# One transformer layer with a routed feed-forward part: another staging of routing, experts and last phase, with GpSimd issuing the experts' row transfers

## The reference

```
h = layernorm(x) * (1 + ca) + sa
x = x + ga * attention(h)                      # one head of 128, softmax over 2048 keys
h = layernorm(x) * (1 + cb) + sb
shared   = (silu(h @ Wg.T) * (h @ Wu.T)) @ Wd.T          # inner width 512
probs    = sigmoid(h @ R.T + bias)             # 8 experts, the two best, scores normed to 1
combined = sum over the two of score_e * expert_e(h)     # each expert like shared, own weights
out = x + gb * (shared + combined)
```

## Time and profile before

| | before |
|---|---|
| median of 3 runs | 1787.32 us |
| profiled execution | 1788.52 us |
| its span, first to last instruction | 1786.8 us |
| TensorE busy | 1645.2 us, 92% |
| VectorE busy | 1046.3 us, 59% |
| ScalarE busy | 826.2 us, 46% |
| GpSimd busy | 497.9 us, 28% |
| granted TensorE clock, mean | 0.965 of full |
| DMA | 134.34 MB, 75 GB/s |

### The profile page before, as it was taken

How to read it: one execution, slowest core, us unless ns; L and a number is a source line. 1 busy time by engine, 2 the same in 40 slices (tenths; PEclk the granted TensorE clock), 3 DMA queues, 4 the chain that set the end, 5 groups by cost and what they waited for, 6 DMA issues and landing times. The chain is left out here.

```text
span 1786.8 us, 34539 instructions
## 1 busy us (share of the span) xinstructions
PE 1645.2 (92%) x10888; PEld 1492.6 (84%) x10889; DVE 1046.3 (59%) x2242; ACT 826.2 (46%) x1628; POOL 497.9 (28%) x504
## 2 busy tenths in 40 slices
PE   8899999999999959897609999999999999988997
PEld 7899999999999848797508888888888888877886
DVE  6777777777778757576533333333333333338987
ACT  5566666565655545455203333333333333335553
POOL 4423223222000030654751020111022400007775
PEclk9999999999999969999859999999999999999999
DMA  3211111111011060211252121122122111114544
GB/s 113 95 43 42 42 42 45 40 47 37 25 37 36 25 230 7 89 73 60 104 192 99 53 88 56 53 91 88 54 90 90 53 53 56 53 43 122 159 144 139
DMA packets 102463, 134.34 MB, mean 75 GB/s; under 512 B 11620, under 2 KB 89572, under 8 KB 102252
## 3 DMA queue, kind: packets, MB, share of 16 engines
q1 hardware_dynamic: 85948, 86.56, 14.8%
q0 software_dynamic: 15312, 44.58, 7.5%
q10 hardware_dynamic: 1120, 2.10, 0.3%
HBM read 79.71 MB, written 53.49 MB: 75 GB/s over the span
## 5 line engine op out<-in xcount | busy, mean ns | idle before, releaser
L794 DVE TENSOR_TENSOR e_aT_lo<-e_bank,e_aT_hi 128x512 fp32r<-128x512 f32 x136 | 94.1, 692 | 239.2 <-ACT e_aT_hi L781 239.2
L757 PE MATMUL e_bank<-e_w_hi,e_xT_hi 128*128 x544 | 225.9, 415 | 0.0
L757 PE MATMUL e_bank<-e_w_hi,e_xT_lo 128*128 x544 | 214.0, 393 | 0.0
L757 PE MATMUL e_bank<-e_w_lo,e_xT_hi 128*128 x544 | 213.3, 392 | 0.0
L800 DVE TENSOR_TENSOR e_prod<-e_silu_g,e_bank 128x512 f32<-128x512 f32 x136 | 93.6, 688 | 189.9 <-PE e_bank L757 189.9
L1394 ACT ACTIVATE e_y<-e_bank 128x256 f32<-128x256 f32 x136 | 52.2, 384 | 320.8 <-PE e_bank L33 320.8
L1565 POOL DMA_INDIRECT y<-y_rows,place_i x128 | 131.7, 1029 | 218.1 <-POOLq L1253 179.4
L608 DVE TENSOR_REDUCE bmax<-s_pair 128x1 f32<-128x512 f32 (+1 forms) x192 | 166.1, 866 | 12.1 <-PE s_pair L33 9.1
L346 ACT ACTIVATE pT_hi<-t_pair 128x512 fp32r<-128x512 f32 (+1 forms) x192 | 136.0, 749 | 78.6 <-PE t_pair L470 76.8
L627 DVE TENSOR_TENSOR pT_lo<-t_pair,pT_hi 128x512 fp32r<-128x512 f32 (+1 forms) x192 | 160.1, 862 | 17.5 <-ACT pT_hi L346 15.5
L339 ACT ACTIVATE prob<-s_pair,negmax 128x1024 f32<-128x1024 f32 x128 | 141.7, 1116 | 57.1 <-DVE negmax L620 51.2
(11 more groups left out here) (294 smaller groups left out, 4562.9 us busy)
## 6 DMA issues: line engine op xcount, KB each, us to landing
e_h<-x_rows SPq DMA_DIRECT2D x136, 128.0 KB, 2.0
y_rows<-e_y SPq DMA_DIRECT2D x136, 128.0 KB, 1.7
XS<-in_x SPq DMA_DIRECT2D x32, 256.0 KB, 2.7
XR<-in_x SPq DMA_DIRECT2D x32, 256.0 KB, 2.6
x<-XR SPq DMA_DIRECT2D x32, 256.0 KB, 2.1
out<-Z SPq DMA_DIRECT2D x16, 512.0 KB
Z<-x SPq DMA_DIRECT2D x2, 2048.0 KB, 15.6
e_w_raw<-in_gate_w POOLq DMA_DIRECT2D x7, 512.0 KB, 4.2
```

The costliest lines, as they stand in the source:

```text
L757: mm = pe.matmul(out[:, 0:I], l, w, start=(c == 0 and k == 0), stop=(c == HC - 1 and k == 2))
L794: dve.tensor_tensor(flat(aT_lo, par), a_bank[:, 0:I], flat(aT_hi, par).bitcast(F32), ALU.subtract).then_inc(f.aT_lo_done, 1)
```

## The change

Attention gets side work. All 27 weight matrices of the feed-forward parts (3 shared, 24 of experts, `piece` = 1024 columns each) are loaded by SP, split by GpSimd and stored, high and low, to HBM (`w_parts`). Statistics are joined on VectorE and made into reciprocal deviations on GpSimd, batch by batch (three of four within attention).

The shared phase loads its split weights. `h` is written by VectorE straight into one of four slots of rows, each row now 260 long: 256 features, the token's number, the place of its first choice, and two numbers for its score. There are eight groups of four steps. Eight further steps with one tile each do the shared part of tiles 32 to 39; within them VectorE makes the plan and SP writes the pad rows and loads the first expert's weights.

In the experts phase SP loads weights already split. GpSimd starts the load of each block's rows and scatters each block's result, in one order. VectorE copies the four extra columns (`rides`) and works out where each result goes and its score (`tell`); ScalarE multiplies by the score as it evicts. Results go to `y_rows` by token, so the last phase reads them with plain DMAs. There, GpSimd adds the two and gates, four tiles at a time, and VectorE adds to the residual; 24 steps remain.

```diff
@@ attention_phase, SP
+            def load_piece(i):
+                if i:
+                    sp.wait_ge(piece_out, 32 * i)
+                sp.dma_start(piece_raw[:], d.matrices[i]).then_inc(piece_in, 16)
+
+            def store_piece(i):
+                sp.wait_ge(piece_split, 2 * i + 2)
+                o = W * (i % 3)
+                for part, src in enumerate((piece_hi[:].bitcast(F32), piece_raw[:])):
+                    sp.dma_start(d.w_parts[i // 3, :, part, o:o + W], src).then_inc(piece_out, 16)
...
             for G in range(ALL):
                 if has_m(G + NG + 3):
                     chunk(G + NG + 3)
+                if 0 <= G - 2 < PIECES:
+                    store_piece(G - 2)
+                if 0 <= G - 1 < PIECES:
+                    load_piece(G - 1)
                 if G >= 2:
                     store(sp, G - 2)
@@ attention_phase, GpSimd
+            def split_piece(i):
+                pool.wait_ge(piece_in, 16 * i + 16)
+                pool.tensor_copy(piece_hi[:], piece_raw[:]).then_inc(piece_split, 1)
+                pool.wait_ge(piece_split, 2 * i + 1)
+                pool.tensor_tensor(piece_raw[:].bitcast(F32R), piece_raw[:], piece_hi[:].bitcast(F32),
+                                   ALU.subtract).then_inc(piece_split, 1)
@@ shared_phase, SP: weights
+            for k in range(3):
...
+                for part in range(2):
+                    o = 3 * W * part + W * k
+                    sp.dma_start(d.w_shared[:, o:o + W].bitcast(F32), d.w_parts[0, :, part, W * k:W * k + W]
+                                 ).then_inc(w_loaded[2 + k], 16)
@@ shared_phase, VectorE
+            def shift(m):
                 dve.wait_ge(scaled_done, m + 1)
...
+                g = m // GS
+                if m < STEPS and m % GS == 0 and g >= RING:
+                    dve.wait_ge(sent[g % RING], ONCE * (g // RING))
+                dve.tensor_tensor(rows_at(m), scaled[:, m % 2, 0:streams(m), :], both_halves(m, H),
                                   ALU.add).then_inc(f.rows_ready, 1)
...
+                if n % GS == 0 and 0 < n <= STEPS:
+                    place(n // GS - 1)
+                if n % GS == GS - 1 and n < STEPS:
+                    choose(n // GS)
+                if n == STEPS:
+                    dve.tensor_copy(free_i[:], base[0:1, GROUPS, :]).then_inc(free_known, 1)
+                if n == STEPS + 2:
+                    plan_ends()
+                if n == STEPS + 3:
+                    plan_experts()
+                if n == STEPS + 4:
+                    plan_rows()
@@ experts_phase, SP
+            for e in range(1, E):
+                if e >= 2:
+
+                    end = sp.value_load(d.ends_i[0:1, e - 2:e - 1], min_val=1, max_val=NBLK)
+                    hold(sp, d, f.y_mm, end)
+                    sp.wait_ge(d.w_ready, 16 * e)
+                sp.dma_start(d.w_all[:, e % 2, :].bitcast(F32), d.w_parts[e + 1].rearrange("p a n -> p (a n)")
+                             ).then_inc(d.w_ready, 16)
@@ experts_phase, GpSimd
+            def scatter(m, par):
+                if inside(m - 1, NBLK):
+                    hold(pool, d, y_sent[1 - par], 16 * half(m - 1, 1 - par) + 16)
+                hold(pool, d, f.y_out, m + 1)
+                pool.indirect_dma_start(d.y_rows, bass.IndirectOffsetOnAxis(ap=goes_to[:, par, :], axis=0),
+                                        y[:, par, :], None).then_inc(y_sent[par], 16)
 
             def load(m, par):
+                row = pool.value_load(d.table[0:1, 0, at(m)], min_val=0, max_val=d.all_rows - P)
+                pool.dma_start(h[:, par, :], d.x_rows[ds(row, P), :]).then_inc(h_in[par], 16)
 
             def step(n, par):
                 if inside(n + 2, NBLK):
+                    pool.wait_ge(ride_done, n + 1)
+                    hold(pool, d, f.xT_mm, n + 1)
                     load(n + 2, par)
                 if inside(n - 2, NBLK):
+                    scatter(n - 2, par)
@@ experts_phase, VectorE, after the products of step n: tell(n - 1), rides(n + 1)
+            def rides(m, par):
...
+                dve.wait_ge(h_in[par], 16 * half(m, par) + 16)
+                dve.tensor_copy(ride[:, par, :], h[:, par, H:H + 4]).then_inc(ride_done, 1)
@@ last_phase, GpSimd
+            for k, q in enumerate(order):
+                y1, y2 = y[:, k % RING, 0, :], y[:, k % RING, 1, :]
+                pool.wait_ge(y_in[k % RING], 32 * (k // RING + 1))
+                pool.tensor_tensor(y1, y1, y2, ALU.add).then_inc(summed, 1)
+                pool.wait_ge(summed, k + 1)
+                pool.tensor_tensor(tiles(y1), tiles(y1), gate_row(C * q).unsqueeze(1).to_broadcast([P, C, H]),
+                                   ALU.mult).then_inc(gated_done, 1)
@@ last_phase, VectorE
+            def output(k):
+
+                q = order[k]
+                dve.wait_ge(gated_done, k + 1)
+                if C * q >= EARLY:
+                    dve.wait_ge(shared_done, C * q - EARLY + C)
+                own = d.Z[:, C * q:C * q + C, :]
+                dve.tensor_tensor(own, own, tiles(y[:, k % RING, 0, :]), ALU.add).then_inc(out_done, 1)
```

More of the change, by code:

```diff
@@ L832, in shared_phase @@
     STEPS = d.steps
-    CHUNK = TB // 2
+    ALL = STEPS + d.extra
+    GROUPS = len(d.groups)
+    GS = STEPS // GROUPS
+    RING = d.ring
+    NBLK = d.blocks
+    W = d.piece
+    ROW = d.row
     Z, rows = d.Z, d.mod_rows
@@ L1174, in choose @@
                 op(dve.reciprocal(two_d(total), two_d(total)))
-                for k, best in enumerate((best1, best2)):
-                    op(dve.tensor_tensor(halves(d.score[:, k, :], first, size), best[:, own], total[:, own], ALU.mult))
+                op(dve.tensor_tensor(two_d(gap), two_d(best1), two_d(best2), ALU.subtract))
+                op(dve.tensor_copy(ride(g, 0), in_group(d.tokens[:], first, size)))
+                op(dve.tensor_tensor(ride(g, 2), best2[:], total[:], ALU.mult))
+                op(dve.tensor_tensor(ride(g, 3), gap[:], total[:], ALU.mult))
                 assert r[0] == ROUTE * g + SCORED
@@ L1226, in _ @@
-            scale(1, 1, 0)
-            shift(1, 1, 0)
-            f.dve_rows_low(dve, 0, 0)
-            for n in range(2, NB):
-                offsets(n, ORDER[n])
-            for g, (first, size) in enumerate(d.groups):
-                now[0] = first // CHUNK
-                pairs(dve, g, step, place)
-                choose(g)
-            place(len(d.groups) - 1)
-            f.dve_products_low(dve, STEPS - 1, 1)
-            for n in (STEPS - 2, STEPS - 1):
-                gated(n, n % 2, n // TB)
-                shared_out(n, n % 2)
@@ L1250, in experts_phase @@
+            f.dve_products_low(dve, ALL - 1, 1)
+            for n in (ALL - 2, ALL - 1):
+                gated(n)
+                shared_out(n)
+def experts_phase(nc, d):
+    E, I, W = d.E, d.I, d.piece
+    H = d.row - 4
+    HC, IC = H // P, I // P
     NBLK = d.blocks
-    W = HC * I
+    T = P * d.NT
     with ExitStack() as ctx:
@@ L1388, in _ @@
+            steps(pool, step)
+            scatter(NBLK - 2, 0)
+            scatter(NBLK - 1, 1)
+            for s in y_sent:
+                pool.wait_ge(s, 16 * (NBLK // 2))
         @block.scalar
@@ L1466, in _ @@
-            op(dve.tensor_reduce(nblocks[:], over[:], AX_X, ALU.add))
-            op(dve.tensor_copy(ends[:], nblocks[:]))
-            for e in range(1, E):
-                op(dve.tensor_tensor(ends[:, e:e + 1], ends[:, e - 1:e], nblocks[:, e:e + 1], ALU.add))
-            op(dve.memset(starts[:, 0:1], 0.0))
-            op(dve.tensor_copy(starts[:, 1:E + 1], ends[:]))
-            op(dve.scalar_tensor_tensor(out=shift[:], in0=starts[:], scalar=-float(P), in1=d.first_row[:, 0:E + 1],
-                                        op0=ALU.mult, op1=ALU.add))
@@ L1509, in _ @@
             f.dve_products_low(dve, NBLK - 1, 1)
+            tell(NBLK - 1, 1)
 def last_phase(nc, d, out):
     H = out.shape[3]
-    I = d.shared_raw[0].shape[2]
+    I, W = d.I, d.piece
     HC, IC = H // P, I // P
     NT, TB = d.NT, d.NT // d.NB
-    EARLY = TB * d.early
+    EARLY = d.steps + d.extra
     LATE = NT - EARLY
-    DEPTH = 4
+    C = 4
+    RING = 12 * W // (2 * C * H)
+    early, late = iter(range(EARLY // C)), iter(range(EARLY // C, NT // C))
+    order = [next(late) if k % 3 == 2 else next(early, None) for k in range(NT // C)]
+    order = [q if q is not None else next(late) for q in order]
     with ExitStack() as ctx:
@@ L1579, in _ @@
+            for k in range(RING):
+                load(k)
+            for k, q in enumerate(order):
+                sp.wait_ge(out_done, k + 1)
+                n = C * q
+                sp.dma_start(out[n // TB, :, n % TB:n % TB + C, :], d.Z[:, n:n + C, :]).then_inc(stored, 16)
+                if k + RING < len(order):
+                    load(k + RING)
+            sp.wait_ge(stored, 16 * len(order))
         @block.scalar
@@ L1736, in constants @@
+            f.dve_products_low(dve, LATE - 1, 1)
```

(22 more changed lines are left out.)

925 lines of the change are left out of this document (409 added, 516 removed).

## The result

The changed kernel takes 1814.86 us (median of 4 runs, 1809.15 to 1815.28), the kernel before 1787.88 in the same comparison: ratio 1.0142, 95% interval 1.012 to 1.0165. The forecast was faster by 1.9%, and the range (1728 to 1788) doesn't hold the time. The profiled execution spans 1813.6 us, 60.2 more than the forecast span of 1753.4.

A forecast was written before the change was run, and what follows sets the result against it. TensorE, busy 92% of the span, was taken to bound the kernel, leaving gains in the gap before the experts and the last phase. Terms summed along product starts cut the span from 1786.8 to 1753.4, giving 1753.9 us, range 1728 to 1788.

The forecast's parts named there:

- Attention: First phase: GpSimd's splitting of 27 weight pieces hides under its waits for ScalarE; 0 us (0 to +3).
- start of the shared phase: Split weights arrive by DMA, so the first product comes 3.1 us sooner, at 651.8; bounds 0 and -5.
- double and single steps: Shared phase: 32 double steps take 215.7 us instead of 218.3; eight added single steps cost +48.7, last product 916.2.
- gap: From the shared phase's last product to the experts' first: 21 us instead of 70.7, first expert product at 937.2.
- routing stalls: Shared phase: each group's routing on VectorE costs 4.2 us; seven in the double steps, 29.4, an eighth in the single steps.
- I take nothing: a load that meets them starts a step early or ends with them.: Experts: row loads meeting the seven 3 MB weight loads (about 7.5 us each) cost nothing; 653.4 us stays (0 to +15).
- The slower rival: Experts: GpSimd's order of loads and scatters sets the step time; up to +90 us, 1844; chance 0.08.
- The rival of late loads: Row loads late beside the weights, or attention hurt by split traffic: +10 to +25, 1764 to 1779; chance 0.12.
- Into the last phase: From the experts' last product to the last phase's first: 26.2 us instead of 19.8, first product at 1616.8.
- the row of the same kind: Shared phase's end today: 11.15 us from GpSimd's last scatter to the next phase, taken for the experts' end, +10.0.
- Half an operation each, 1.1 x 32 = 36. Of this VectorE hides 0.9 a step, 21 in all: 15.: Last phase: GpSimd's 32 adding and gating operations hold VectorE up, 15 us on top of 111.3 for 24 steps.
- The rival that it stands beside: Last phase: full exclusion of VectorE and GpSimd, 36 us more than the forecast, 1790, level with today; chance 0.12.

The follow-up runs named there:

- weights paced: Changed kernel, each next expert's 3 MB of weights sent as six loads of 512 KB, each begun when the one before has landed: 1778.3 us.
- rows a step sooner: Changed kernel with four slots for the experts' rows instead of two, GpSimd loading block n + 3 in step n, weights still 3 MB at once: 1774.3 us.
- small pieces: Changed kernel, GpSimd adding and gating in the last phase in pieces of 256 columns instead of 1024: 1786.3 us.
- five of six runs: Changed kernel with rows three steps ahead, weights in chained pieces, GpSimd's 256-column pieces and normalised rows in PSUM: 1756.1 us, these five between 1751.8 and 1758.0.
- another kernel: Changed kernel with rows three steps ahead, weights in chained pieces, GpSimd's 256-column pieces, normalised rows in SBUF, no GpSimd wait for VectorE: 1743.4 us.

## Why the prediction was wrong, by its own steps

- **Attention, start of the shared phase, double and single steps, gap.** Right in sum, 936.6 against 937.2, in part because two errors cancel. GpSimd's split stayed under cover (its wait for ScalarE fell from 306.6 us to 228.4). The double steps lost 3.2 us less than forecast, mostly because two of the seven routing stalls cost 2.7 us and not 4.2. The first rows, issued 1.5 us behind 3 MB of weights, took 8.0 us to land where 5 to 6 were priced, the same error as in the experts; with the weights paced the first product came 5.5 us sooner.
- **"I take nothing: a load that meets them starts a step early or ends with them."** This step failed, for 41.2 us. 3 MB took 10.9 us, not the 7.5 scaled from loads of 512 KB, and rows issued 1.5 us behind them took 7.7 (7.5 to 8.1 at all six places), three times the median and beyond the worst landing of the trace before (5.7). That worst landing lay beside 1.5 MB, in three transfers; beside twice the bytes in one it was no upper bound. The slack of 1.3 us that the working found was right (3.7 us from issue to need, 2.4 to land); paced weights (-31.6) and rows a step sooner (-39.3) show that it was what lacked. And a wait of 4.1 us costs 6.8, 2.7 of it at half clock.
- **The slower rival** (GpSimd's order as the clock of the experts, late in every step) didn't happen: between the weight loads the steps are 4.85. The rival of late loads named the mechanism but priced it at 10 to 25.
- **Into the last phase.** From the end of GpSimd's last scatter to the next phase it took 6.3 us (1638.8 to 1645.1), not the 11.15 of the row of the same kind, which is 4.9 less; 1.1 came back because the last scatter waited for the landing of the one before, and 0.4 elsewhere, so 3.4 remain.
- **"Half an operation each, 1.1 x 32 = 36. Of this VectorE hides 0.9 a step, 21 in all: 15."** The second step that failed, for 22.9 us. The waits sum to 43.3 (0.564 + 0.566 + 0.535 over 24 steps, 0.207 over 16 chunks), near the 36; what failed is the hiding. Slack is per step, and GpSimd works in bursts: one of 14 operations, then three of six (three chunks) with 8 to 12 us between, in which it waits for loads. In the step shown above four operations wait 1.0, 2.2, 1.8 and 2.1 us, 7.1 in one step, and the two steps of 4.9 in each four have little to hide. Of 43.3 us 5.6 were hidden (37.7 lost, the half clock among them). With small pieces it is 28.2 and 11.3 are lost, so 17 hidden. That the trace before could not show the reverse was right: there GpSimd did gathers in this phase and no arithmetic, and beside them the 64 additions with both inputs in SBUF kept their length:

```profile
L1685 DVE TENSOR_TENSOR Z<-l_gated,Z x64: 412/420/427, 1619.1 to 1783.1; 128x256 f32<-128x256 f32 x64
```

- On this the Trainium skill (SBUF — State Buffer, "Who interferes with whom") was right against my reading of the trace: whole operations, in both directions. The rival that it stands beside (1790, so 162 us for the last phase) was nearer in this term than my 126.3; measured were 149.2. The 23 us show one thing more: the loser need not be next in line.
- The range failed because both mishaps had a rival each and none held the two together; they lie in different phases and add up. The late rows alone, 41.2 us on 1753.9, would have left it too; the last phase's 22.9 alone would not.

## What to carry to other kernels

A transfer of a few us issued behind megabytes of others is late by a good part of their time (here 5.3 us behind 10.9): ask at every large load which small ones come behind it and how many us they have, and either begin them a step sooner (more slots) or send the large one in pieces that wait for each other. Slack hides waits step by step, never by their sum: find out whether the engine that causes them works in bursts. Before work goes from VectorE to GpSimd, list VectorE's operations with both inputs in SBUF beside it; each may wait for a whole GpSimd operation, so keep those short, put an input in PSUM, and give GpSimd, once its operations are short, a wait on VectorE's progress.

## What the runs showed of the hardware

- A VectorE addition took 23.07 us instead of 0.42, while 33 GpSimd operations of 0.7 us ran; the times of five of six runs fit such a stall, that of the sixth (1735.2) doesn't. In another kernel 128 GpSimd operations in a row held no addition over 1.61 us.
- VectorE's operations with one input in PSUM keep 0.41 us beside a busy GpSimd; those with two in SBUF reach 2.6. GpSimd's own operations of 1024 columns last 2.3 to 3.3 us beside them.
- 130 KB beside 3 MB: up to 8.3 us issued by GpSimd, up to 10.2 by ScalarE, 6.3 beside the same bytes as six transfers, 4.4 at most beside chained pieces of 512 KB; 2.4 and 2.1 in the median of all.
- An idle stretch of 4.1 us on TensorE came with half clock from its middle on (0.53 over the 7 us from 1042), and 2.7 us more than the wait itself were lost.
